# One ring of eight PSUM banks and new engine orders in the middle layers of a four-stage transformer kernel

## The chip, the cores and the metric

One core of a Trainium2 chip runs the whole program. The metric is the device time of one execution in microseconds, the median of several runs. A core has a matrix engine (TensorE, PE in the rows), VectorE (DVE), ScalarE (ACT), GpSimd (POOL) and SyncE (SP), which only issues transfers here. TensorE writes its products to PSUM, a memory of eight banks; VectorE and ScalarE read them there, and only then can a bank be written again.

## The reference

Two sequences of 2048 tokens of width 256 go through four blocks; everything is float32. The middle two blocks, which the change touches, are one function applied twice with other weights:

```python
def _layer(x, wqkv, qs, ksc, wo, lg, lb, w1, b1, w2, b2):
    h = shift_token(x)                      # right half of the features one token later
    q, k, v = jnp.split(h @ wqkv, 3, axis=-1)        # 8 heads of 64
    q = l2norm(q) * qs
    k = l2norm(k) * ksc
    q, k = rotary_xpos(q, k)
    o = local_attention(q, k, v)            # each 128-token window sees itself and the last one
    x = x + o @ wo
    h = layernorm(shift_token(x)) * lg + lb
    a, g = jnp.split(h @ w1 + b1, 2, axis=-1)        # 682 each
    return x + (a * gelu(g)) @ w2 + b2
```

Ahead of them stands an attention layer with 16 narrow heads and its own feed-forward, behind them a gated attention unit and a matmul with ternary weights.

## The kernel before

Each block is a phase of its own, with all engines joined at its end. The middle layers are the function `layer_b`, built once and run twice by a hardware loop. It walks over 16 tiles of 128 tokens (`t`), for both sequences (`b` is 0 or 1). To keep float32 accuracy TensorE forms most products as three: each operand is split in a high and a low part (`product3`, lines 113 to 115). The split of an operand that comes out of PSUM takes one operation on ScalarE (`_hi`) and one on VectorE (`_lo`), so nearly every matmul result is read by both.

The work of a tile is cut into stages, and every engine has its own list of them, `order[engine]`, with entries (stage, batch or part, shift). `in_turns` runs such a list once per turn i; an entry handles tile i + shift, and is left out where that tile doesn't exist. So a turn has work of up to six tiles in it, and the list is the order of the engine's instructions, fixed when the program is built. The stages on TensorE are: `turn_h` transposes the input; `project_k`, `project_q`, `project_v` are the three projections (6 matmuls of 512 columns each); `turn_qk` transposes k and q; `scores` and `scores2` form the scores of the first and the second four heads (64 rows are contracted, two matmuls side by side, 12 in all for each stage); `turn_p` and `turn_p2` transpose the probabilities; `values` multiplies them with v; `turn_o` and `out` bring the result through the output weights; `turn_f`, `up` 0 to 5 and `down` are the feed-forward. 33 entries and 344 matmuls stand in a full turn. Between them work, among others: on ScalarE the squares of q and k (L1242), the exponentials (L1273), the gelu of `up` (L1307) and the `_hi` parts; on VectorE `sums` (L1334), `spin` (the rotation, L1346 and L1348), the masked maxima of the scores (L1378), copies of the turned probabilities (L1399), `up` (L1449) and `mid` (L1458), the moments and the normalisation; on GpSimd the inverse norms by a power (L1195, L1209) and the sums and products on k and q (L1198 to L1206). SyncE issues the transfers to and from memory.

The exponential and the gelu need different function tables on ScalarE. Where one follows the other, the built program has an ACT_TABLE_LOAD.

The banks are given out by `Ring`. It numbers its uses in the order of TensorE's list, and use n lies in bank n modulo the ring's length. `wait_bank` makes TensorE wait until the use before in the same bank is drained; `written` and `read` count up the bank's two semaphores. Before the change there are two rings:

```python
main = Ring(sem, psum, f"{name}_main", range(0, 6), [(t, (job, b)) for stage, t, b in turns(order["pe"], NT) ...])
ffn = Ring(sem, psum, f"{name}_ffn", range(6, 8), [(t, (f_jobs[stage], b)) for stage, t, b in turns(order["pe"], NT) ...])
```

`main` holds the 36 uses of attention in a turn: h, k, q, v, kT, qT, four of scores (s), four of turned probabilities (p), two of values (o), oT and wo, each for both batches. `ffn` holds nine: f, w0 to w5 and y for both batches.

Of the kernel before, what the change touches and what calls it, by code (L numbers as in the profile page):

```python
# [906 lines left out]
def layer_b(nc, io, psum, sem, layer):  # L907
# [11 lines left out]
        "pe": [("scores", 0, -1), ("up", 0, -3), ("up", 1, -3), ("project_v", 1, -1), ("turn_h", 0, 0), ("turn_qk", 1, -1),
               ("out", 1, -2), ("scores2", 0, -1), ("down", 0, -4), ("down", 1, -4), ("scores", 1, -1), ("turn_p", 0, -1),  # L920
               ("up", 2, -3), ("scores2", 1, -1), ("turn_p2", 0, -1), ("project_k", 0, 0), ("values", 0, -1),
               ("turn_p", 1, -1), ("up", 3, -3), ("turn_h", 1, 0), ("project_q", 0, 0), ("up", 4, -3), ("turn_p2", 1, -1),
               ("project_k", 1, 0), ("turn_o", 0, -1), ("values", 1, -1), ("up", 5, -3), ("turn_qk", 0, 0),
               ("project_q", 1, 0), ("turn_f", 0, -2), ("project_v", 0, 0), ("out", 0, -1), ("turn_o", 1, -1)],
        "dve": [("up", 5, -4), ("turn_qk", 0, -1), ("turn_f", 0, -3), ("sums_q", 1, -1), ("spin_q", 1, -1), ("out", 0, -2),
               ("mid", 4, -4), ("turn_o", 1, -2), ("scores", 0, -1), ("mid", 5, -4), ("up", 0, -3), ("turn_h", 0, 0),
               ("up", 1, -3), ("turn_qk", 1, -1), ("out", 1, -2), ("scores2", 0, -1), ("down", 0, -4), ("scores", 1, -1),
               ("turn_p", 0, -1), ("scores2", 1, -1), ("down", 1, -4), ("mid", 0, -3), ("moments", 0, -2), ("sums_k", 0, 0),
               ("spin_k", 0, 0), ("up", 2, -3), ("values", 0, -1), ("turn_h", 1, 0), ("turn_p", 1, -1), ("sums_q", 0, 0),
               ("spin_q", 0, 0), ("mid", 1, -3), ("sums_k", 1, 0), ("up", 3, -3), ("spin_k", 1, 0), ("norm", 0, -2),  # L930
               ("mid", 2, -3), ("up", 4, -3), ("mid", 3, -3), ("turn_o", 0, -1), ("values", 1, -1)],
        "sp": [("out", 1, -2), ("scores2", 0, -1), ("residual", 1, -1), ("rope", 0, 0), ("load_r", 0, -3),
               ("residual", 0, -1), ("load_f", 0, -2), ("load_f", 1, -2), ("scores2", 1, -1), ("values", 1, -1),
               ("load_r", 1, -3), ("values", 0, -1), ("down", 0, -4), ("down", 1, -4), ("out", 0, -1)],
        "pool": [("moments", 0, -3), ("project_k", 0, -1), ("project_q", 0, -1), ("project_k", 1, -1), ("load_r", 0, -4),
                ("project_q", 1, -1), ("rope", 0, 0)],
    }
# [1511 lines left out]
```

How the kernel before makes its waits and increments, by code:

```python
    def wait_bank(self, eng, it, job):  # L63
        bank, use = self.place[job]
        eng.wait_ge(self.drained[bank], it * self.uses[bank] + use)
# [1 line left out]
    def wait_before(self, eng, it, job):  # L67
        bank = self.place[job][0]
        eng.wait_ge(self.drained[bank], it * self.uses[bank])
# [1 line left out]
    def wait_before_full(self, eng, it, job):  # L72
        bank = self.place[job][0]
        eng.wait_ge(self.full[bank], it * self.uses[bank])
# [1 line left out]
    def wait_full(self, eng, it, job):  # L77
        bank, use = self.place[job]
        eng.wait_ge(self.full[bank], it * self.uses[bank] + use + 1)
# [1 line left out]
    def wait_drained(self, eng, it, job):  # L81
        bank, use = self.place[job]
        eng.wait_ge(self.drained[bank], it * self.uses[bank] + use + 1)
# [18 lines left out]
    def link(self, ins):  # L102
        self.n += 1
        ins.then_inc(self.sem, 1)
        self.eng.wait_ge(self.sem, self.it * self.per_step + self.n)
# [42 lines left out]
    def wait_bank(self, eng, t, job):  # L148
        bank, use = self.place[t, job]
        if use > 0:
            eng.wait_ge(self.drained[bank], use)
# [1 line left out]
    def wait_full(self, eng, t, job):  # L153
        bank, use = self.place[t, job]
        eng.wait_ge(self.full[bank], use + 1)
# [1 line left out]
    def wait_drained(self, eng, t, job):  # L157
        bank, use = self.place[t, job]
        eng.wait_ge(self.drained[bank], use + 1)
# [24 lines left out]
    def link(self, ins):  # L184
        self.n += 1
        ins.then_inc(self.sem, 1)
        self.eng.wait_ge(self.sem, self.n)
# [555 lines left out]
        @block.tensor  # L743
        def _(pe):
            pe.wait_ge(consts_ready, n_consts + 1)
```

## Time and profile before

| | |
|---|---|
| median of 3 runs | 2870.94 us (2868.68 to 2872.28) |
| the profiled execution | 2867.2 us |
| its span, first to last instruction | 2865.4 us |
| granted clock of TensorE, mean | 0.954 of 2.4 GHz |
| busy: TensorE, VectorE, ScalarE, GpSimd | 2633.9, 2071.1, 1449.6, 1022.7 us |
| first layer | 0 to about 589 us |
| middle layers, weights and ramps included | about 589 to 1323 and 1323 to 2060 us |
| gated unit and ternary matmul | the rest |

Busy times of the engines overlap. A TensorE that counts as busy all the time can still lose time, since matmuls overlap in their pipeline: what it gets done shows in the distances between their starts, and the views below are read that way.

### The profile page before, as it was taken

To read this page: it belongs to the slowest core of one execution; us is meant where nothing else is said; L and a number is where in the kernel's file an instruction comes from. 1 tells how busy PE (TensorE), PEld (TensorE's weight loads), DVE (VectorE), ACT (ScalarE), POOL (GpSimd) and SP (SyncE) were. 2 spreads that over 40 slices of the span, in tenths; PEclk is the share of its full clock that TensorE was granted. 3 is DMA by queue.
4 is the path that set the end of the run, shared out by engine and by line. 5 is a ranking of instruction groups with operands and counts; after the bars stand their busy time and mean duration, and the time that the engine had idled before them with its cause. 6 is when DMAs were issued, how large, how long until landed. Compare 5 with 4: busy or idle time off the path is not lost. (4 is left out here: it accounts for less than half of the span.)

```text
span 2865.4 us, 57375 instructions
## 1 busy us (share of the span) xinstructions
PE 2633.9 (92%) x20450; PEld 2383.0 (83%) x20450; DVE 2071.1 (72%) x6161; ACT 1449.6 (51%) x3028; POOL 1022.7 (36%) x906
## 2 busy tenths in 40 slices
...
GB/s 71 32 33 41 33 33 33 33 99 89 64 87 79 77 78 79 84 79 90 75 79 87 66 90 78 76 80 73 108 129 98 23 30 30 71 128 30 30 30 23
DMA packets 223102, 189.55 MB, mean 66 GB/s; under 512 B 22357, under 2 KB 204505, under 8 KB 221913
## 3 DMA queue, kind: packets, MB, share of 16 engines
...
q8 instruction: 169, 2.77, 0.4%
...
## 5 line engine op out<-in xcount | busy, mean ns | idle before, releaser
L2147 ACT ACTIVATE c_sb_kern_hi<-c_sb_kern 128x512 fp32r<-128x512 f32 x128 | 80.9, 632 | 427.5 <-DVE c_sb_kern L2167 427.5
L2124 POOL TENSOR_TENSOR c_sb_kern_lo<-c_sb_kern,c_sb_kern_hi 128x512 fp32r<-128x512 f32 x128 | 166.8, 1304 | 313.4 <-ACT c_sb_kern_hi L2147 313.4
L2163 DVE SCALAR_TENSOR_TENSOR c_sb_kern<-psum,cu_bias 128x512 f32<-128x512 f32 x128 | 88.4, 690 | 245.8 <-PE psum L115 244.2
L1273 ACT ACTIVATE b_sb_probs<-b_sb_probs,b_sb_neg_top,b_sb_r_norm 128x256 f32<-128x256 f32 x512 | 262.3, 589 | 1.0 <-DVE b_sb_neg_top L1385 0.5
L1378 DVE CUSTOM_DVE_ANT_0 b_sb_probs<-psum,b_sb_mask 128x256 f32<-128x256 f32 x512 | 194.9, 417 | 65.0 <-PE psum L1520 64.0
L113 PE MATMUL psum<-b_sb_fT_lo,b_sb_w_hi 128*128 128x256 f32 x768 | 227.2, 296 | 4.1 <-DVE b_sb_fT_lo L1443 2.8
L115 PE MATMUL psum<-b_sb_fT_hi,b_sb_w_hi 128*128 128x256 f32 x768 | 216.5, 282 | 0.0
L114 PE MATMUL psum<-b_sb_fT_hi,b_sb_w_lo 128*128 128x256 f32 x768 | 215.8, 281 | 0.0
L113 PE MATMUL psum<-c_sb_kern_lo,cu_v_hi 128*128 128x512 f32 x512 | 206.9, 404 | 2.9 <-POOL c_sb_kern_lo L2124 2.9
L115 PE MATMUL psum<-c_sb_kern_hi,cu_v_hi 128*128 128x512 f32 x512 | 204.0, 398 | 0.0
L114 PE MATMUL psum<-c_sb_kern_hi,cu_v_lo 128*128 128x512 f32 x512 | 203.5, 398 | 0.0
L1565 PE MATMUL psum<-b_sb_v_now,b_sb_pT 128*128 128x65 f32 x1024 | 198.0, 275 | 0.0
L1564 PE MATMUL psum<-b_sb_v_prev,b_sb_pT 128*128 128x65 f32 x1024 | 194.5, 272 | 0.0
L1307 ACT ACTIVATE b_sb_gate<-psum,b_sb_b 128x256 f32<-128x256 f32 x192 | 91.0, 475 | 173.6 <-PE psum L115 162.2
L1206 POOL TENSOR_TENSOR b_sb_qk_cos<-b_sb_qk_cos,b_sb_qk_sin 128x512 f32<-128x512 f32 x64 | 82.2, 1284 | 250.2 <-DVEq L1350 250.2
L113 PE MATMUL psum<-b_sb_w_lo,b_sb_hT_hi 128*128 128x512 f32 x384 | 166.2, 433 | 4.5 <-DVE b_sb_hT_lo L1327 4.2
L1564 PEld LDWEIGHTS psum<-b_sb_v_prev,b_sb_pT 128*128 128x128 f32 x1024 | 157.7, 192 | 2.8
L507 ACT ACTIVATE a_probs<-a_probs,a_neg_top 128x128 f32<-128x128 f32 x512 | 155.1, 392 | 5.7 <-DVE a_neg_top L649 5.5
L1565 PEld LDWEIGHTS psum<-b_sb_v_now,b_sb_pT 128*128 128x128 f32 x1024 | 155.5, 192 | 0.0
L113 PEld LDWEIGHTS psum<-b_sb_fT_lo,b_sb_w_hi 128*128 128x128 f32 x768 | 144.7, 188 | 10.2 <-DVE b_sb_fT_lo L1443 3.3
L114 PE MATMUL psum<-b_sb_w_hi,b_sb_hT_lo 128*128 128x512 f32 x384 | 152.7, 398 | 0.0
L115 PE MATMUL psum<-b_sb_w_hi,b_sb_hT_hi 128*128 128x512 f32 x384 | 152.7, 398 | 0.0
...
## 6 DMA issues: line engine op xcount, KB each, us to landing
...
Y<-b_sb_y SPq DMA_DIRECT2D x128, 128.0 KB, 1.7
b_sb_h_in<-Y ACTq DMA_DIRECT2D x128, 64.0 KB, 1.9
...
b_sb_x_f<-Y SPq DMA_DIRECT2D x128, 64.0 KB, 2.1
...
```

The lines of the kernel that those rows point to most:

```text
L113: pe.matmul(out, w_hi, x_lo, start=first, stop=False)
L114: pe.matmul(out, w_lo, x_hi, start=False, stop=False)
L115: return pe.matmul(out, w_hi, x_hi, start=False, stop=last)
L507: ins = act.activation(probs[b][:, h, :], probs[b][:, h, :], ACT.Exp, bias=neg_top[b][:, h:h + 1], scale=float(A_HD) ** -0.5)
L1206: pool.tensor_tensor(q, q, qk_sin[b][:, 0, :, :], ALU.add).then_inc(qk_ready[b], 1)
L1273: ins = act.activation(probs[b][:, n, :], probs[b][:, n, :], ACT.Exp, bias=neg_top[b][:, n:n + 1], scale=r_norm[b][:, h:h + 1])
L1307: act.activation(gate[m % 2][:], ffn.out(t, ("w", m), 512)[:, 0:256], ACT.Gelu, bias=b1[:, 2 * m:2 * m + 1])\
L1378: ins = dve.tensor_tensor_reduce(out=probs[b][:, n, :], in0=main.out(t, (f"s{m}", b), 512)[:, j * 256:(j + 1) * 256], in1=mask[:, min(t, 1 ...
L1564: pe.matmul(out, pT[b][:, 2 * slot, :], v_prev[b][:, h, :], start=True, stop=False)
L1565: ins = pe.matmul(out, pT[b][:, 2 * slot + 1, :], v_now[b][:, h, :], start=False, stop=True)
L2124: pool.tensor_tensor(kern_lo[n][:], kern[n][:], kern_hi[n][:].bitcast(F32), ALU.subtract)\
L2163: sbanks.read(dve.scalar_tensor_tensor(out=kern[n][:], in0=sbanks.out((t, j), C_CHUNK), scalar=float(C_S) ** -0.5, in1=unit.bias[:, at:at ...
```

## The change

All of it lies in `layer_b`. The two rings become one of eight banks, numbered through all 45 uses of a turn in TensorE's order, and each call of `main` or `ffn` becomes one of `ring`. No stage is added, removed or changed, and no operation on data. The five lists of orders are other ones: the entries are the same, but their places and shifts differ. The core of the diff:

```diff
-               ("scores", 0, -2), ("mid", 0, -4), ("scores2", 0, -2), ("scores", 1, -2), ("mid", 1, -4), ("turn_p2", 0, -2),
+               ("mid", 5, -4), ("scores", 0, -1), ("up", 0, -3), ("up", 1, -3), ("scores2", 0, -1), ("mid", 0, -3),
...
-        "pe": [("scores", 0, -1), ("up", 0, -3), ("up", 1, -3), ("project_v", 1, -1), ("turn_h", 0, 0), ("turn_qk", 1, -1),
...
+        "pe": [("down", 1, -5), ("scores", 1, -2), ("scores2", 1, -2), ("turn_p", 0, -2), ("turn_p2", 0, -2),
...
-        f_jobs = {"turn_f": "f", "up": "w", "down": "y"}
-        main = Ring(sem, psum, f"{name}_main", range(0, 6), [(t, (job, b)) for stage, t, b in turns(order["pe"], NT)
-                                                             if stage in jobs for job in jobs[stage]])
-        ffn = Ring(sem, psum, f"{name}_ffn", range(6, 8), [(t, (f_jobs[stage], b)) for stage, t, b in turns(order["pe"], NT)
-                                                           if stage in f_jobs])
+        jobs.update(turn_f=["f"], up=["w"], down=["y"])
+        ring = Ring(sem, psum, f"{name}_ring", range(8), [(t, (job, b)) for stage, t, b in turns(order["pe"], NT)
+                                                          if stage in jobs for job in jobs[stage]])
```

The whole turn on TensorE now reads: `down` 1, `scores` 1, `scores2` 1, `turn_p` 0, `turn_p2` 0, `project_k` 0, `up` 2, `turn_p` 1, `project_q` 0, `up` 3, `values` 0, `turn_p2` 1, `project_k` 1, `values` 1, `turn_o` 0, `project_q` 1, `project_v` 0, `up` 4, `turn_o` 1, `turn_qk` 0, `project_v` 1, `turn_h` 0, `up` 5, `turn_f`, `turn_h` 1, `out` 1, `scores` 0, `turn_qk` 1, `scores2` 0, `out` 0, `up` 0, `up` 1, `down` 0.

TensorE, at the scores of batch 1, in a full turn (numbers behind names are the batch). Before, they stand between `down` of batch 1 and the turned probabilities of batch 0, and `up` 2 follows:

```order
L115 MATMUL psum<-b1_sb_w2_hi,b1_sb_mid_hi 128x256
L1520 MATMUL psum<-b1_sb_kT_lo1,b1_sb_qT_hi1 128x256 x2
L1520 MATMUL psum<-b1_sb_kT_hi1,b1_sb_qT_lo1 128x256 x2
L1520 MATMUL psum<-b1_sb_kT_hi1,b1_sb_qT_hi1 128x256 x2
L1520 MATMUL psum<-b1_sb_kT_lo1,b1_sb_qT_hi1 128x256 x2
L1520 MATMUL psum<-b1_sb_kT_hi1,b1_sb_qT_lo1 128x256 x2
L1520 MATMUL psum<-b1_sb_kT_hi1,b1_sb_qT_hi1 128x256 x2
L1541 MATMUL psum<-b1_sb_ident,b1_sb_probs0 128x128 x8
L113 MATMUL psum<-b1_sb_fT_lo,b1_sb_w1_hi 128x256
L114 MATMUL psum<-b1_sb_fT_hi,b1_sb_w1_lo 128x256
L115 MATMUL psum<-b1_sb_fT_hi,b1_sb_w1_hi 128x256
```

After, the rows begin inside the first of two scores stages of batch 1 and end with the projection of k:

```order
L1519 MATMUL psum<-b1_sb_kT_hi1,b1_sb_qT_lo1 128x256 x2
L1519 MATMUL psum<-b1_sb_kT_hi1,b1_sb_qT_hi1 128x256 x2
L1519 MATMUL psum<-b1_sb_kT_lo1,b1_sb_qT_hi1 128x256 x2
L1519 MATMUL psum<-b1_sb_kT_hi1,b1_sb_qT_lo1 128x256 x2
L1519 MATMUL psum<-b1_sb_kT_hi1,b1_sb_qT_hi1 128x256 x2
L1519 MATMUL psum<-b1_sb_kT_lo1,b1_sb_qT_hi1 128x256 x2
L1519 MATMUL psum<-b1_sb_kT_hi1,b1_sb_qT_lo1 128x256 x2
L1519 MATMUL psum<-b1_sb_kT_hi1,b1_sb_qT_hi1 128x256 x2
L1540 MATMUL psum<-b1_sb_ident,b1_sb_probs0 128x128 x16
L113 MATMUL psum<-b1_sb_w_lo,b1_sb_hT_hi0 128x512
```

The second four heads' scores moved up to the first four's, and both halves of batch 0's probabilities are turned behind them.

ScalarE, from the exponentials of batch 0 on. Before:

```order
L1273 ACT_TABLE_LOAD
L1273 ACTIVATE b_sb_probs<-b_sb_probs,b_sb_neg_top,b_sb_r_norm 128x256 x4
L1314 ACTIVATE b_sb_mid_hi<-b_sb_mid 128x256
L1273 ACTIVATE b_sb_probs<-b_sb_probs,b_sb_neg_top,b_sb_r_norm 128x256 x8
L1314 ACTIVATE b_sb_mid_hi<-b_sb_mid 128x256
L1287 ACTIVATE b_sb_pT<-psum 128x512 x2
L1242 ACTIVATE b_sb_qk_sin<-psum 128x512
L1273 ACTIVATE b_sb_probs<-b_sb_probs,b_sb_neg_top,b_sb_r_norm 128x256 x4
L1307 ACT_TABLE_LOAD
L1307 ACTIVATE b_sb_gate<-psum,b_sb_b 128x256
L1235 ACTIVATE b_sb_hT_hi<-psum 128x256
```

After:

```order
L1272 ACT_TABLE_LOAD
L1272 ACTIVATE b_sb_probs<-b_sb_probs,b_sb_neg_top,b_sb_r_norm 128x256 x4
L1306 ACT_TABLE_LOAD
L1306 ACTIVATE b_sb_gate<-psum,b_sb_b 128x256 x2
L1272 ACT_TABLE_LOAD
L1272 ACTIVATE b_sb_probs<-b_sb_probs,b_sb_neg_top,b_sb_r_norm 128x256 x4
L1313 ACTIVATE b_sb_mid_hi<-b_sb_mid 128x256
L1272 ACTIVATE b_sb_probs<-b_sb_probs,b_sb_neg_top,b_sb_r_norm 128x256 x8
L1241 ACTIVATE b_sb_qk_sin<-psum 128x512
L1313 ACTIVATE b_sb_mid_hi<-b_sb_mid 128x256
L1286 ACTIVATE b_sb_pT<-psum 128x512 x2
```

The first two gelus of `up` moved between the two halves of batch 0's exponentials, with a table load on either side.

VectorE, around the sums and the spin of batch 0's k (`squares0`, `qk_cos0`). Before:

```order
L1458 TENSOR_TENSOR b1_sb_mid_lo<-b1_sb_mid0,b1_sb_mid_hi 128x256
L1427 BN_STATS b1_sb_stats<-b1_sb_x_f 128x6 x2
L1430 BN_AGGR b1_sb_mv<-b1_sb_stats 128x2 x2
L1432 TENSOR_SCALAR b1_sb_var<-b1_sb_mv 128x2
L1334 TENSOR_REDUCE b1_sb_squares0<-b1_sb_qk_sin0 128x8
L1335 TENSOR_SCALAR b1_sb_squares0<-b1_sb_squares0 128x8
L1346 TENSOR_TENSOR b1_sb_qk_sin0<-psum,b1_sb_rope 128x8x32 x2
L1348 TENSOR_TENSOR b1_sb_qk_cos0<-psum,b1_sb_rope 128x512
L1449 SCALAR_TENSOR_TENSOR b1_sb_mid0<-psum,b1_sb_b1,b1_sb_gate0 128x256
```

After:

```order
L1333 TENSOR_REDUCE b1_sb_squares0<-b1_sb_qk_sin0 128x8
L1334 TENSOR_SCALAR b1_sb_squares0<-b1_sb_squares0 128x8
L1345 TENSOR_TENSOR b1_sb_qk_sin0<-psum,b1_sb_rope 128x8x32 x2
L1347 TENSOR_TENSOR b1_sb_qk_cos0<-psum,b1_sb_rope 128x512
L1457 TENSOR_TENSOR b1_sb_mid_lo<-b1_sb_mid0,b1_sb_mid_hi 128x256
L1426 BN_STATS b1_sb_stats<-b1_sb_x_f 128x6 x2
L1429 BN_AGGR b1_sb_mv<-b1_sb_stats 128x2 x2
L1431 TENSOR_SCALAR b1_sb_var<-b1_sb_mv 128x2
L1448 SCALAR_TENSOR_TENSOR b1_sb_mid0<-psum,b1_sb_b1,b1_sb_gate0 128x256
```

The low part of `mid` and the moments moved from ahead of the sums to behind the spin, ahead of `up` 2.

## Rows read from the trace of the kernel before

**Rows 1.** Busy time by stretches: stretch, length, busy us (instructions) of each engine, clock, DMA.
```profile
612.00:700.00 88.00, 73.83 (x538) 63.55 (x539) 67.01 (x206) 43.56 (x82) 48.98 (x42) 0.92 0.21 65
700.00:1250.00 550.00, 549.26 (x4449) 512.30 (x4447) 467.31 (x1350) 331.43 (x640) 221.82 (x169) 1.00 0.25 78
1250.00:1323.00 73.00, 61.56 (x522) 59.37 (x520) 39.08 (x110) 29.37 (x62) 5.37 (x5) 0.97 0.21 65
```

**Rows 2.** Waits of TensorE, 700 to 1250 us: total, times, longest.
```profile
PE psum L1541 <- ACT b_sb_probs L1273: 0.7, 2, 0.4
```

**Rows 3.** Timeline of TensorE: start, us, line, operation, shapes, count.
```profile
904.26 0.38 PE L1520 MATMUL psum<-b_sb_kT_lo,b_sb_qT_hi 64*128 64x256 f32 x2
...
911.90 0.28 PE L115 MATMUL psum<-b_sb_wo_hi,b_sb_oT_hi 128*128 128x256 f32 x1
912.11 0.39 PE L1520 MATMUL psum<-b_sb_kT_lo,b_sb_qT_hi 64*128 64x256 f32 x2
912.33 0.28 PE L1520 MATMUL psum<-b_sb_kT_hi,b_sb_qT_lo 64*128 64x256 f32 x2
...
912.81 0.28 PE L1520 MATMUL psum<-b_sb_kT_hi,b_sb_qT_hi 64*128 64x256 f32 x2
913.02 0.39 PE L113 MATMUL psum<-b_sb_w_lo,b_sb_mid_hi 128*128 128x256 f32 x1
913.24 0.28 PE L114 MATMUL psum<-b_sb_w_hi,b_sb_mid_lo 128*128 128x256 f32 x1
...
924.08 0.33 PE L1564 MATMUL psum<-b_sb_v_prev,b_sb_pT 128*128 128x65 f32 x2
...
927.60 1.04 PE L1541 MATMUL psum<-b_sb_ident,b_sb_probs 128*128 128x128 f32 x8
```

**Rows 4.** The same view, one turn later.
```profile
946.71 0.39 PE L1520 MATMUL psum<-b_sb_kT_lo,b_sb_qT_hi 64*128 64x256 f32 x2
```

**Rows 5.** The same view, in the ramp of the first middle layer.
```profile
670.93 0.28 PE L1520 MATMUL psum<-b_sb_kT_hi,b_sb_qT_hi 64*128 64x256 f32 x2
671.05 0.29 PE L1520 MATMUL psum<-b_sb_kT_lo,b_sb_qT_hi 64*128 64x256 f32 x2
671.18 0.28 PE L1520 MATMUL psum<-b_sb_kT_hi,b_sb_qT_lo 64*128 64x256 f32 x2
```

**Rows 6.** Groups of VectorE, 750 to 1200 us: busy, mean ns, idle before.
```profile
L1378 DVE CUSTOM_DVE_ANT_0 b_sb_probs<-psum,b_sb_mask 128x256 f32<-128x256 f32 x166 | 63.1, 417 | 24.6 <-PE psum L1520 24.3
L1458 DVE TENSOR_TENSOR b_sb_mid_lo<-b_sb_mid,b_sb_mid_hi 128x256 fp32r<-128x256 f32 x64 | 46.2, 722 | 4.3 <-DVE b_sb_mid L1449 2.7
L1346 DVE TENSOR_TENSOR b_sb_qk_sin<-psum,b_sb_rope 128x256 f32<-128x256 f32 x86 | 32.2, 416 | 2.6 <-DVE b_sb_mid L1449 2.6
L1449 DVE SCALAR_TENSOR_TENSOR b_sb_mid<-psum,b_sb_b,b_sb_gate 128x256 f32<-128x256 f32 x64 | 30.7, 480 | 13.4 <-ACT b_sb_gate L1307 12.7
L1348 DVE TENSOR_TENSOR b_sb_qk_cos<-psum,b_sb_rope 128x512 f32<-128x512 f32 x43 | 29.2, 679 | 0.0
L1334 DVE TENSOR_REDUCE b_sb_squares<-b_sb_qk_sin 128x8 f32<-128x512 f32 x43 | 29.2, 678 | 0.4
L1399 DVE COPY b_sb_pT<-psum 128x512 f32<-128x512 f32 x44 | 28.2, 681 | 0.0
```

**Rows 7.** Timelines of VectorE and GpSimd (POOL).
```profile
918.61 0.42 DVE L1378 CUSTOM_DVE_ANT_0 b_sb_probs<-psum,b_sb_mask 128x256 f32<-128x256 f32 x1 [2.38 <-PE psum L1520]
...
934.69 1.28 POOL L1206 TENSOR_TENSOR b_sb_qk_cos<-b_sb_qk_cos,b_sb_qk_sin 128x512 f32<-128x512 f32 x1 [4.10 <-DVEq L1350]
...
934.70 1.55 DVE L1458 TENSOR_TENSOR b_sb_mid_lo<-b_sb_mid,b_sb_mid_hi 128x256 fp32r<-128x256 f32 x1
```

**Rows 8.** Timeline of ScalarE, a table switch and what follows.
```profile
911.96 1.28 ACT L1273 ACT_TABLE_LOAD   x1
913.25 2.08 ACT L1273 ACTIVATE b_sb_probs<-b_sb_probs,b_sb_neg_top,b_sb_r_norm 128x256 f32<-128x256 f32 x4
...
926.91 1.28 ACT L1307 ACT_TABLE_LOAD   x1
```

More of the change, by code:

```diff
@@ L919, in layer_b @@
-        "pe": [("scores", 0, -1), ("up", 0, -3), ("up", 1, -3), ("project_v", 1, -1), ("turn_h", 0, 0), ("turn_qk", 1, -1),
[L920 to L936, printed above, removed]
+        "act": [("turn_p2", 0, -2), ("up", 2, -4), ("load", 0, 0), ("load", 1, 0), ("project_q", 0, -1), ("up", 3, -4),
+               ("turn_p2", 1, -2), ("project_k", 1, -1), ("turn_o", 0, -2), ("project_q", 1, -1), ("project_v", 0, -1),
+               ("turn_o", 1, -2), ("mid", 2, -4), ("turn_qk", 0, -1), ("up", 4, -4), ("turn_h", 0, 0), ("project_v", 1, -1),
+               ("mid", 3, -4), ("turn_h", 1, 0), ("turn_f", 0, -3), ("up", 5, -4), ("mid", 4, -4), ("turn_qk", 1, -1),
+               ("mid", 5, -4), ("scores", 0, -1), ("up", 0, -3), ("up", 1, -3), ("scores2", 0, -1), ("mid", 0, -3),
+               ("scores", 1, -1), ("scores2", 1, -1), ("project_k", 0, 0), ("mid", 1, -3)],
@@ new lines, in layer_b @@
+        "pe": [("down", 1, -5), ("scores", 1, -2), ("scores2", 1, -2), ("turn_p", 0, -2), ("turn_p2", 0, -2),
+               ("project_k", 0, -1), ("up", 2, -4), ("turn_p", 1, -2), ("project_q", 0, -1), ("up", 3, -4),
+               ("values", 0, -2), ("turn_p2", 1, -2), ("project_k", 1, -1), ("values", 1, -2), ("turn_o", 0, -2),
+               ("project_q", 1, -1), ("project_v", 0, -1), ("up", 4, -4), ("turn_o", 1, -2), ("turn_qk", 0, -1),
+               ("project_v", 1, -1), ("turn_h", 0, 0), ("up", 5, -4), ("turn_f", 0, -3), ("turn_h", 1, 0), ("out", 1, -2),
+               ("scores", 0, -1), ("turn_qk", 1, -1), ("scores2", 0, -1), ("out", 0, -2), ("up", 0, -3), ("up", 1, -3),
+               ("down", 0, -4)],
```

221 lines of the change are left out of this document (114 added, 107 removed).

## Prediction

> **What bounds the kernel now.** I read the busy time by stretches first. The middle layers run twice, at about 612 to 1323 and 1346 to 2050 us. Between the ends of the first one TensorE is busy 549.3 of 550 us at a granted clock of 1.00, the full 2.4 GHz, while VectorE works 467 and ScalarE 331 [rows 1]. The waits of that stretch hold one entry for TensorE, 0.7 us in all [rows 2]. So nothing but TensorE sets the pace there. The same group of matmuls, scores of batch 0, begins at 904.26 and at 946.71 [rows 3, 4]: a turn, one step of 128 tokens of both batches, takes 42.45 us, and 16 of them 679 us. A change of the banks cannot win back waits that are not there. What can be won in a full turn is the time that TensorE loses between its own groups; what can be won elsewhere lies at the two ends of a layer, where TensorE is idle 88 - 73.8 = 14.2 us (part of it before the first load has landed) and 73 - 61.6 = 11.4 us [rows 1].
>
> **Where TensorE loses time between groups.** The scores contract over 64 rows, all else over 128. Inside a run of 256-column matmuls the starts are 0.12 apart. From the last `out` matmul at 911.90 to the first scores pair at 912.11 it is 0.21, and from that to the second pair at 912.33 it is 0.22; leaving, 912.81 to 913.02 is 0.21 and the next step, to 913.24, 0.22 [rows 3]. So entering costs 0.09 + 0.10 and leaving 0.09 + 0.10: 0.19 each way. In the ramp of the layer two scores groups do stand next to each other: 670.93, 671.05, 671.18 are 0.12 and 0.13 apart [rows 5], so joined groups pay nothing at the seam. The Trainium skill ("TensorEngine Tiling (Array Packing)", Tiling Modes, Key Properties) says that changing the tiling mode, not just the tile, drains TensorE; these rows agree in kind and give the size.
>
> **Part one, the order on TensorE.** Before, the four scores groups of a turn stand alone: four entries, four exits. After, scores and scores2 of batch 1 follow each other between `down` and the turning of the probabilities: three entries and three exits. The lost pair is one entry from and one exit to full-row matmuls, 0.19 + 0.19 = 0.38 us in a turn. The matmuls themselves are the same 344 in a turn; the other seams change place and I cost them at 0, plus or minus 0.05. 32 turns by 0.38 = 12.2 us less. All of it lies on the path, since TensorE is the path.
>
> **Part two, the ring.** Now use n waits until use n-8 is drained, whatever it is, where projections and attention had six and the feed-forward two. With 45 uses a turn this is no new work, but it ties the chains of the feed-forward to the attention. I walked one turn by the new order with TensorE never waiting, time 0 at the start of `down` of batch 1, with group lengths from TensorE's timeline (values 924.08 to 927.60 = 3.52, a scores group 912.11 to 913.02 = 0.91 [rows 3], the others likewise). VectorE, one engine in order, gets the scores of batch 1 at 3.3. Two sets of four (0.42 each [rows 6], with the small ones about 1.8 a set) bring it to 6.9, the two copies for batch 0 (0.61 apart, 0.68 long [rows 6]) to 8.1. The copies of batch 1 wait for TensorE's turning, written at 9.2, and end at 10.4. Sums of squares (0.68 and a short one) to 11.2; spin, twice 0.42 and 0.68 and its signal, to 12.8; `mid` 0 to 14.2 (below); moments, about 1.1, to 15.3; `up` 2, 0.48, to 15.8 [rows 6]. The bank of w2 is the one that p3 of batch 1 takes eight uses later, and TensorE wants that at 16.1: a margin of 0.3 us, the smallest in the turn. Next are h of batch 1 after w4 (about 31.0 against 30.3: 0.7), scores of batch 0 after kT and qT (32.7 against 31.8: 0.9), and some of 1 to 2 us. So I take no wait: 0. The other end is all of these late by the one thing that I can size badly, below.
>
> **VectorE's room.** In the old turn it waits 2.38 us at 918.61 for the scores [rows 7] and some 1.1 us elsewhere; in the new one a turn is 0.38 shorter and its work the same, so about 3 us stay. One cost moves: at 934.70 a `mid` subtraction takes 1.55 us where the undisturbed ones take 0.42, because a GpSimd addition began at 934.69 and lasted 1.28 [rows 7]; the mean over the stretch is 0.72 [rows 6]. The new order puts `mid` 0 behind spin_k of batch 0, exactly the place where spin lets the GpSimd addition start, and I have counted 1.1 us for it in the 15.8. The wide normalisation keeps its place behind a spin.
>
> **Part three, ScalarE.** The new order puts `up` 0 and 1 between the exponentials of batch 0's two halves: four table switches in a turn in place of two, at 1.28 us [rows 8]: +2.6 us a turn. ScalarE is busy 331 of 550 us [rows 1], 25.6 in a turn; 28.2 of 42 is still no bound. What hangs on it: the exponentials of scores2 of batch 0, done by 2.4 in my walk and wanted by TensorE at 5.2; and `up` 2, which ScalarE has ready at about 11.8, while VectorE comes to it at 15.3. Both are covered, with 2.8 and 3.5 us; beyond that each us late is a us per turn. In the trace the exponential starts 1.29 after its load began, at once [rows 8]. The Trainium skill ("ScalarE: Activation LUTs", What ACT_TABLE_LOAD costs) adds a drain of about 1380 ns to each switch and tells to do all of one set before the next; by it the extra would be 5.3 us a turn and the cover of 2.8 would be nearly gone, so it speaks against this change. The sum goes by the rows, where the drain isn't seen.
>
> **The ends of a layer.** The first turn of the new order turns both h before the first projection, so the projection of k of batch 1 doesn't wait for VectorE; but the chain through spin, GpSimd and the k and q turning is as long as before. From walking it I take 1 us less a layer, between 4 less and 3 more, of the 25.6 idle [rows 1]. The last turns hold the same `turn_f` to `up` seam as before: 0.
>
> **SyncE and GpSimd.** Their orders change, but each transfer in my walk lands well ahead (k and v are moved about 20, wanted at 27): 0. Outside the middle layers nothing moves.
>
> **The sum.** The profiled execution took 2867.2 us (span 2865.4), 3.7 under the median of 2870.9 of three runs. 2867.2 - 12.2 - 2 by 1 = 2853.0; against the median, 2856.7, or 0.5% less.
>
> **Rivals.**
> - *A bank comes late in every turn (slower).* w2's drain passes 16.1. The cause would be a second block of VectorE by a GpSimd addition in the chain from 3.3 to 15.8, at 1.1 us (1.55 - 0.42 [rows 7]). As VectorE waits for TensorE again at the next `down`, the wait recurs in all turns. One block more: 1.1 - 0.3 = 0.8 us a turn, less the 0.38: +0.42 by 32 = +13 us, less the 2 at the ends: 2882 us; it decides from a chain 0.7 us longer than mine. For it: margins of 0.3 and 0.7 are thin and eight banks now tie everything. Against: the GpSimd additions fall behind the spins only, and between 9.2 and 10.4 VectorE waited anyway. The same price, at 2.8 us, would hold for ScalarE's late exponentials.
> - *Small waits eat the gain (same).* The chain is late by 0.5 us: 0.2 us a turn is lost, 6 us back: 2863, or with 0.4, 2869.
> - *The seam isn't saved.* The 0.12 of the joined pair is seen in one ramp turn of each layer; where the second group has to wait for a bank just drained the seam stays at 0.2. Then only half or none of 12.2 comes: 2863 to 2869.
> - *The ends give more.* If the two feed-forward banks held the ramp up, up to 5 us a layer go: 2847.
>
> **How the numbers follow.** Forecast 0.62 (2850 to 2862). Small waits or a seam not saved 0.20, of which half falls within 0.2% (5.7 us, about what a measurement can tell here from no change) of 2870.9. The ends give more 0.07. A bank late in every turn 0.11. Faster by more than that: 0.62 + 0.10 + 0.07 = 0.79; same 0.10; slower 0.11. The range goes from the ends giving more, 2846, to small waits eating all, 2869.
>
> **What the profile after would show.** Right: full turns 42.0 to 42.1 apart at clock 1.00; no wait of TensorE between them; in the scores of batch 1 starts 0.12 apart through all twelve pairs; 60 more ACT_TABLE_LOADs, about 77 us more of ScalarE, waited for by nobody. Wrong: a repeated TensorE wait for `b_sb_mid` L1448 at the turning of the probabilities (a bank), or for `b_sb_probs` (exponentials late), once a turn; or seams of 0.2 inside the joined pair.

## The result

| | before | after |
|---|---|---|
| median | 2874.36 us (2868.68 to 2877.38, 8 runs) | 2862.84 us (2858.58 to 2865.82, 8 runs) |
| profiled execution | 2867.2 us | 2859.99 us |
| its span | 2865.4 us | 2858.2 us |

The ratio of after to before is 0.996, with a 95% interval of 0.9949 to 0.9971: the changed kernel is faster by 0.4%, some 11.5 us. The forecast was 14 us less, 2857, in a range of 2846 to 2869.

The busy times in the middle of the first layer, the same view as [rows 1] (stretch, length, busy us of each engine, granted clock, DMA):

```profile
700.00:1250.00 550.00, 548.93 (x4495) 515.51 (x4493) 458.82 (x1372) 359.93 (x668) 210.80 (x168) 1.00 0.25 78
```

TensorE is the bound as before, 548.9 of 550 us at full clock. But in the same 550 us it now has 4495 matmuls in place of 4449: 1% more of its work. Its waits, 720 to 1250 us (total, times, longest):

```profile
PE psum L1480 <- DVE b_sb_mid L1448: 0.2, 1, 0.2
```

One wait in twelve turns. The joined scores of batch 1 in TensorE's timeline (start, us, line, operation, shapes, count), with the first matmul of the same group one turn later:

```profile
918.41 0.28 PE L115 MATMUL psum<-b_sb_w_hi,b_sb_mid_hi 128*128 128x256 f32 x1
918.62 0.39 PE L1519 MATMUL psum<-b_sb_kT_lo,b_sb_qT_hi 64*128 64x256 f32 x2
918.84 0.28 PE L1519 MATMUL psum<-b_sb_kT_hi,b_sb_qT_lo 64*128 64x256 f32 x2
...
919.20 0.28 PE L1519 MATMUL psum<-b_sb_kT_hi,b_sb_qT_lo 64*128 64x256 f32 x2
919.32 0.28 PE L1519 MATMUL psum<-b_sb_kT_hi,b_sb_qT_hi 64*128 64x256 f32 x2
...
920.04 0.28 PE L1519 MATMUL psum<-b_sb_kT_hi,b_sb_qT_hi 64*128 64x256 f32 x2
920.25 1.97 PE L1540 MATMUL psum<-b_sb_ident,b_sb_probs 128*128 128x128 f32 x16
...
960.67 0.39 PE L1519 MATMUL psum<-b_sb_kT_lo,b_sb_qT_hi 64*128 64x256 f32 x2
```

The entry is there (0.21, 0.22) and the exit (0.21), and in between all steps are 0.12: the second group, which begins at 919.32, pays neither. The turn is 960.67 - 918.62 = 42.05 us, against 42.45 [rows 3, 4]; over seven turns of each the difference is 0.407.

The length of a layer is read from the start of its first matmul to that of its last. After:

```profile
621.29 0.45 PE L1480 MATMUL psum<-b_sb_ident,b_sb_h_in 128*128 128x128 f32 x1 [8.46 <-DMA b_sb_h_in<-Y]
...
1310.43 0.28 PE L115 MATMUL psum<-b_sb_w_hi,b_sb_mid_hi 128*128 128x256 f32 x1
...
1351.07 0.45 PE L1480 MATMUL psum<-b_sb_ident,b_sb_h_in 128*128 128x128 f32 x1 [8.61 <-DMA b_sb_h_in<-Y]
...
2039.21 0.28 PE L115 MATMUL psum<-b_sb_w_hi,b_sb_mid_hi 128*128 128x256 f32 x1
```

Before, the same four:

```profile
619.66 0.66 PE L1481 MATMUL psum<-b_sb_ident,b_sb_h_in 128*128 128x128 f32 x2 [8.58 <-DMA b_sb_h_in<-Y]
...
1313.82 0.28 PE L115 MATMUL psum<-b_sb_w_hi,b_sb_mid_hi 128*128 128x256 f32 x1
...
1352.33 0.45 PE L1481 MATMUL psum<-b_sb_ident,b_sb_h_in 128*128 128x128 f32 x1 [8.55 <-DMA b_sb_h_in<-Y]
...
2046.42 0.28 PE L115 MATMUL psum<-b_sb_w_hi,b_sb_mid_hi 128*128 128x256 f32 x1
```

The first layer went from 694.16 to 689.14 us (-5.0), the second from 694.09 to 688.14 (-6.0), -11.0 together, close to the 11.5 between the medians. 16 turns by 0.407 would be -6.5 in each, so the ends gave back 1.5 and 0.5. The stretch between the layers, in which the weights are loaded, was 38.5 us before and 40.6 after, and the first layer began 1.6 us later. In the traces of the other kernels, whatever their orders, the stretch took 39.0 to 41.1 us and the first layer began at 617.2 to 624.0, so I take both for the spread of single executions. They are why the profiled execution came out only 7.2 us shorter (11.0 - 2.1 - 1.6).

### The profile page after: what moved, and what is told of

It is laid out like the page before. It is cut to its first block and busy times, and to the rows that moved or that the text cites. A ratio compares the mean times of both kernels' runs of the same rounds, so it can differ in the third digit from the quotient of the medians.

```text
span 2858.2 us, 57407 instructions
## 1 busy us (share of the span) xinstructions
PE 2624.7 (92%) x20450; PEld 2385.3 (83%) x20450; DVE 2046.6 (72%) x6161; ACT 1501.8 (53%) x3080; POOL 1000.6 (35%) x906
## 5 line engine op out<-in xcount | busy, mean ns | idle before, releaser
L1194 POOL TENSOR_TENSOR b_sb_r_norm<-b_sb_squares,b_sb_power 128x8 f32<-128x8 f32 x64 | 105.0, 1641 | 643.8 <-DVE b_sb_squares L1334 643.8
L113 PE MATMUL psum<-b_sb_fT_lo,b_sb_w_hi 128*128 128x256 f32 x768 | 218.9, 285 | 2.9 <-DVE b_sb_fT_lo L1442 2.9
L114 PEld LDWEIGHTS psum<-b_sb_fT_hi,b_sb_w_lo 128*128 128x128 f32 x768 | 144.6, 188 | 3.5
```

Source lines behind the costliest of these rows:

```text
L113: pe.matmul(out, w_hi, x_lo, start=first, stop=False)
L114: pe.matmul(out, w_lo, x_hi, start=False, stop=False)
L1194: pool.tensor_tensor(r, s, p, ALU.pow).then_inc(r_ready[1][b], 1)
```

## The experiments

Two questions: is the one saved seam the whole gain, and what do the ring and the other orders do? The theory is that the seam is all of it and the ring gives nothing of itself; the rival, that the shared banks take waits away.

**x1_split: the changed kernel without the joined pair.**

```diff
-        "pe": [("down", 1, -5), ("scores", 1, -2), ("scores2", 1, -2), ("turn_p", 0, -2), ("turn_p2", 0, -2),
+        "pe": [("down", 1, -5), ("scores", 1, -2), ("turn_p", 0, -2), ("scores2", 1, -2), ("turn_p2", 0, -2),
```

> The changed kernel with one thing undone: on TensorE scores2 of batch 1 goes back behind the turning of the first half of batch 0's probabilities, so the two scores groups stand apart again. Ring of eight and all other orders stay. Theory (the seam is the whole gain): one entry and one exit come back, 0.38 us a turn, a full turn 42.43 in place of 42.05, 32 turns: +12.2 us, so about 2862.8 + 12.2 = 2875, level with the kernel before. Rival (the gain came from the ring and the new orders taking waits away elsewhere): a turn stays near 42.05 and the time near 2863.

Measured 2872.79 us; ratio to before 1.000 (0.9991 to 1.001). TensorE's timeline, the first group of the pair in two turns:

```profile
878.45 0.39 PE L1519 MATMUL psum<-b_sb_kT_lo,b_sb_qT_hi 64*128 64x256 f32 x2
...
920.85 0.39 PE L1519 MATMUL psum<-b_sb_kT_lo,b_sb_qT_hi 64*128 64x256 f32 x2
```

A turn takes 42.40 us, 0.35 more than after, and all of the gain is gone. This is also the price of everything else in the change, the ring, the two more table loads of ScalarE and the five new lists: 42.40 against 42.45, nothing that the times can tell. Its layers took 694.67 and 694.05 us, those of the kernel before 694.16 and 694.09.

**x2_join_only: the kernel before with the joined pair.**

```diff
-               ("out", 1, -2), ("scores2", 0, -1), ("down", 0, -4), ("down", 1, -4), ("scores", 1, -1), ("turn_p", 0, -1),
-               ("up", 2, -3), ("scores2", 1, -1), ("turn_p2", 0, -1), ("project_k", 0, 0), ("values", 0, -1),
+               ("out", 1, -2), ("scores2", 0, -1), ("down", 0, -4), ("down", 1, -4), ("scores", 1, -1), ("scores2", 1, -1),
+               ("turn_p", 0, -1), ("up", 2, -3), ("turn_p2", 0, -1), ("project_k", 0, 0), ("values", 0, -1),
```

> The kernel before with one thing done: on TensorE scores2 of batch 1 is moved up behind scores of batch 1. Two rings of six and two and all the other lists as before. Theory (seam): the turn falls from 42.45 to 42.07, 32 turns: -12.2 us, so 2874.4 - 12.2 = 2862, as good as the changed kernel without any ring of eight. VectorE waits for the turned probabilities of batch 0 up to 0.9 us longer, inside the 2.4 us that it waits there anyway. Rival (the joined groups need the new ring or the new VectorE order, else a bank comes late): the gain is eaten, 2868 to 2880, and a repeated TensorE wait shows at the turned probabilities.

Measured 2875.26 us; ratio 1.001 (1.0001 to 1.0019). The theory alone is wrong here: the seam inside the pair is saved, but the full turns vary from 42.35 to 42.83 and average 42.50. TensorE's timeline shows what eats it, at the projection of k of batch 0, in two turns:

```profile
971.81 0.47 PE L113 MATMUL psum<-b_sb_w_lo,b_sb_hT_hi 128*128 128x512 f32 x1 [0.47 <-ACT b_sb_pT L1287]
...
1014.33 0.47 PE L113 MATMUL psum<-b_sb_w_lo,b_sb_hT_hi 128*128 128x512 f32 x1 [0.16 <-DVE b_sb_top L1378]
```

and VectorE's timeline why: the maxima of the second pair (L1378), which drain s2's bank, come behind the two copies.

```profile
969.70 1.28 DVE L1399 COPY b_sb_pT<-psum 128x512 f32<-128x512 f32 x2
...
971.24 0.42 DVE L1378 CUSTOM_DVE_ANT_0 b_sb_probs<-psum,b_sb_mask 128x256 f32<-128x256 f32 x1
```

In a ring of six, k of batch 0 takes the bank of s2 of batch 1, drained at 971.24 + 0.42 = 971.66; k starts at 971.81. (The first of the two waits is put down to ScalarE; the second names the maxima.) The turns in which the profile shows no wait lose by it too: at 928.97 this projection starts 0.26 us after the start of the last turned probability, where in the kernel before it is 0.03. That is too small to show as idle, since one matmul's time overlaps the next.

**x2b_join_dve: the same, with VectorE's scores2 of batch 1 ahead of the copies.**

```diff
-               ("turn_p", 0, -1), ("scores2", 1, -1), ("down", 1, -4), ("mid", 0, -3), ("moments", 0, -2), ("sums_k", 0, 0),
+               ("scores2", 1, -1), ("turn_p", 0, -1), ("down", 1, -4), ("mid", 0, -3), ("moments", 0, -2), ("sums_k", 0, 0),
```

> The kernel before with two things done: scores2 of batch 1 behind scores of batch 1 on TensorE (as in the run x2_join_only), and the same on VectorE, ahead of the copies of the turned probabilities. Still two rings of six and two. Theory (x2_join_only lost its 0.38 us because s2 of batch 1, whose bank k of batch 0 takes six uses later, was drained behind the copies): the bank comes 1.4 us earlier, the wait at the projection of k goes, a full turn is 42.07, 32 turns: -12 us against before, about 2860. Rival (six banks can't carry the joined pair): the wait stays or moves to the values, the turn stays 42.4 to 42.5 and the time at 2871 to 2875.

Measured 2879.55 us; ratio 1.0029 (1.0019 to 1.0039): slower than before. The wait at the projection is gone, as the theory had it, and the quietest turns are 42.14, 0.31 under the kernel before, where 42.07 was expected. But the copies are now later than `values` wants them (a TensorE wait of 0.3 us for `b_sb_pT` L1399 in the trace), so the turns reach 42.7, and the ramp and the last turns lose more than the full ones gain: turns 1 and 2 (a layer's first is turn 0) take 31.1 and 31.4 us in place of 30.2 and 30.2, turn 16 takes 35.1 and 38.4 in place of 34.1. So the small edit isn't the change. The saved seam needs the engines' orders around it; whether some other order on two rings would carry it is not tested.

**x3_ring8_old: the one ring of eight with the old orders** (against the kernel before, the lists of uses cut).

```diff
-        main = Ring(sem, psum, f"{name}_main", range(0, 6), [...])
-        ffn = Ring(sem, psum, f"{name}_ffn", range(6, 8), [...])
+        ring = Ring(sem, psum, f"{name}_ring", range(8), [...])
```

> The one ring of eight with the five old lists of orders. From the times of the kernel before, each use's start against the drain of the use eight places earlier: four places a turn would be late, p2 of batch 0 behind y of batch 1 by 2.3 us, o0 of batch 1 behind w3 by 1.8, p0 of batch 1 behind w2 by 1.7, kT of batch 0 behind w4 by 1.1. Theory (the ring gives nothing by itself and needs other orders): TensorE waits at these places, 2.3 us a turn if one wait shifts the others away and 4 if half of them remain: +75 to +130 us, about 2950 to 3000. Rival (the ring alone is harmless or helps): within 5 us of the kernel before.

Measured 3116.37 us; ratio 1.0853 (1.0836 to 1.087). Slower than the forecast of at most 3000 by 116 us. TensorE's waits over some eleven turns, 720 to 1250 us:

```profile
PE psum L1539 <- DVE b_sb_y L1463: 24.1, 10, 2.4
PE psum L1562 <- DVE b_sb_mid L1447: 19.6, 11, 1.8
PE psum L1539 <- DVE b_sb_mid L1447: 16.7, 10, 1.7
```

Three of the four late places are there with the sizes read from the margins of before (2.4, 1.8, 1.7 against 2.3, 1.8, 1.7), and none covers another: 5.9 us a turn. The fourth, at kT, doesn't show. Between the starts of the matmuls the three places cost 6.2 us a turn (why that is more than the waits shown is told in the last section). The rest is the clock: by stretches, the granted clock (third column from the end) falls behind the third wait to its lower level of 1.2 GHz, for 6.8 us in all:

```profile
870.00:880.00 10.00, 8.22 (x60) 7.44 (x59) 7.71 (x15) 4.72 (x10) 4.26 (x3) 1.00 0.05 13
880.00:885.00 5.00, 5.00 (x28) 5.00 (x28) 4.50 (x11) 0.00 (x0) 3.04 (x3) 0.56 0.02 5
885.00:890.00 5.00, 5.00 (x28) 4.64 (x28) 1.94 (x4) 2.12 (x5) 1.29 (x1) 0.76 0.53 187
```

The full turns take about 50.3, 52.0 or 54.8 us, and in the clock's records of these turns it stands at 1.2 GHz for 3.4 us behind the second wait, for 6.8 behind the third, and in the longest for 13.7 in three pieces. 42.45 + 6.2 is 48.7; the 1.6, 3.3 and 6.1 us above it go with the lower clock.

**x4_rings62_new: the new orders on the two old rings** (the swap, against the changed kernel's list for VectorE).

```diff
-               ("down", 0, -4), ("up", 0, -3), ("up", 1, -3), ("down", 1, -4), ("scores", 1, -1), ("scores2", 1, -1),
+               ("up", 0, -3), ("up", 1, -3), ("down", 0, -4), ("down", 1, -4), ("scores", 1, -1), ("scores2", 1, -1),
```

> The new lists of orders on the two old rings, with one swap on VectorE without which two banks can't carry them: up 0 and up 1 go ahead of down of batch 0, since y of batch 0 now waits for the bank of w0. Theory (the new orders need the shared banks): y of batch 0 begins when VectorE has used w0, at about 915.75 in place of 914.26 of the changed kernel's turn, 1.5 us late each turn; k of batch 0 waits for s2 of batch 1 some 0.4 more. Turn 43.6 to 44.0, +50 to +60 us against the changed kernel, 2910 to 2925. Rival (the ring is not needed): the turn stays at 42.05 and the time at 2863.

Measured 2925.0 us; ratio 1.0179 (1.0162 to 1.0196). TensorE's waits:

```profile
PE psum L113 <- DVE b_sb_mid L1450: 14.7, 12, 1.3
PE psum L113 <- DVE b_sb_top L1379: 2.7, 12, 0.2
PE psum L1521 <- DVE b_sb_y L1423: 2.1, 12, 0.2
```

Once a turn each: y of batch 0 for w0's bank (14.7 / 12 = 1.2 us, where 1.5 was forecast), k for s2's, and s3 for wo's, which was not foreseen. The turn is 44.17, a little over the 43.6 to 44.0 expected, and the time is at the upper edge of its range. These orders cost 1.8% on two rings, and by x3_ring8_old the ring costs 8.5% with the old orders. Together they come to zero, and leave room for the joined pair.

**z1_vector_1us: how much room is there for a late bank?** The changed kernel with work added on VectorE:

```diff
                 dve.wait_ge(mid_hi_ready, t * B_FC + m + 1)
+                for k in range(3 if m == 0 else 0):
+                    dve.tensor_reduce(scratch[k][:], mid[m % 2][:], AX.X, ALU.add)
```

> The changed kernel with three sums of a 128x256 tile added on VectorE ahead of the subtraction of mid 0 (their results go nowhere), some 0.35 us each, 1.05 in all: the one block more of the prediction's slower rival. By the prediction's walk the bank of w2 had 0.3 us to spare: 0.75 us a turn, +24 us, 2887. By the drains seen in the trace after, w2's bank has 1.5 us to spare and the smallest margins are h of batch 1 after w4 with 0.8, and kT, qT for the scores of batch 0 with 1.0: 0.3 us a turn, +9 us, about 2872, with the wait at the turning of h. If VectorE's room takes it up before: 2863.

Measured 2875.5 us; ratio to before 1.0009 (0.9996 to 1.0022), by the ratios some 14 us more than after. TensorE's timeline at the turning of h of batch 1, after first and then this run, and the run's waits:

```profile
946.93 0.60 PE L1590 MATMUL psum<-b_sb_ident,b_sb_xn 128*128 128x128 f32 x4
947.36 0.38 PE L1480 MATMUL psum<-b_sb_ident,b_sb_h_in 128*128 128x128 f32 x2
...
947.80 0.60 PE L1593 MATMUL psum<-b_sb_ident,b_sb_xn 128*128 128x128 f32 x4
948.56 0.41 PE L1483 MATMUL psum<-b_sb_ident,b_sb_h_in 128*128 128x128 f32 x2 [0.16 <-DVE b_sb_mid L1449]
```

```profile
PE psum L1483 <- DVE b_sb_mid L1449: 2.0, 12, 0.2
```

The wait comes where the drains of the trace had it, at h after w4, in each turn, and not at w2's bank. The turns are 42.49 us. The wait itself shows 0.16 and the turn grew by 0.44: 0.33 at this place (0.76 from start to start in place of 0.43) and the rest at the turning of the probabilities.

The edit did somewhat more than 1.05 us at first. The three sums took 0.99, and behind them the subtraction of `mid` 0 started while GpSimd's addition ran and in most turns took 0.91 us in place of 0.43, so VectorE came 1.4 us later to `up` 2, which drains w2's bank; from `mid` 1 on it was 1.0 behind. That w2's bank still came in time says that its margin was at least 1.4.

**z2_two_loads: what is left of ScalarE's cover?** The changed kernel with one more switch there and back:

```diff
             def up(t, m):
+                if m == 1:
+                    act.activation(scratch[:], ident[:, 0:1], ACT.Exp)
```

> The changed kernel with an exponential of one column added on ScalarE between up 0 and up 1, which brings two more table loads, 2.56 us and some 0.2 each for the small ones, to where the change had put two: it asks how much of the cover is left, and whether a switch costs more than its load. In the trace after, the exponentials of scores2 of batch 0 end 2.2 us before TensorE turns them. Theory (a switch costs its 1.28 us alone): 2.8 - 2.2 = 0.6 us a turn, and up 1 comes about as late for VectorE: +20 us, 2883. Rival (by the Trainium skill, ScalarE: Activation LUTs, a drain of about 1380 ns goes with each switch): 2 x 1.38 more, 3.4 us a turn, +108 us, 2971.

Measured 2882.47 us; ratio 1.0034 (1.0023 to 1.0045). ScalarE's timeline:

```profile
966.06 1.28 ACT L1306 ACT_TABLE_LOAD   x1
967.35 0.20 ACT L1306 ACTIVATE b_sb_scratch<-b_sb_ident 128x1 f32<-128x1 f32 x1
967.56 1.28 ACT L1309 ACT_TABLE_LOAD   x1
968.86 0.47 ACT L1309 ACTIVATE b_sb_gate<-psum,b_sb_b 128x256 f32<-128x256 f32 x1
969.35 1.28 ACT L1273 ACT_TABLE_LOAD   x1
```

Each load takes 1.28 us, what follows starts within 0.02, and each load starts within 0.02 of the end before it. The drain that the Trainium skill ("ScalarE: Activation LUTs", What ACT_TABLE_LOAD costs) puts beside each switch isn't in this trace, and the time is nowhere near the 2971 that it would have given. The turn is 42.40, TensorE waits 0.2 us a turn for the exponentials (L1273) and each full turn is 0.35 longer: of the 2.8 us added ScalarE's cover took some 2.4. Turn 4 of the layers, the last before the full ones, grew by 5.2 and 4.1 us: TensorE waits 3.5 us there in place of 0.6, and behind that wait the granted clock stood at 1.2 GHz for 6.8 and 3.4 us.

**r1_ramp, y2_join_both, y4_mixed, y5_mixed_ramp: the ends, and more of the same.**

r1_ramp moves one entry on VectorE, in the first turn of a layer:

```diff
+            steps.remove(("turn_qk", 0, 0))
+            steps.insert(steps.index(("sums_q", 0, 1)), ("turn_qk", 0, 0))
```

> The changed kernel with one thing moved in the first turn of a layer: on VectorE the low parts of kT and qT of batch 0 of the first tile come ahead of the sums and spin of q of batch 1. It takes away the longest wait in the ramp: TensorE stood 2.8 us, from 636.1 to 638.9, ahead of the first scores. Theory A (that wait is what the ends lost): the first scores come at about 636.8, 2.1 us less a layer, 4 us in all, 2859 in place of 2863. Theory B (the ramp is set by GpSimd's chain of k and q of batch 1, whose last sum ends at 640.7 whatever VectorE does): the wait moves to the turning of k and q of batch 1, the first scores of batch 1 stay within 0.4 us of 22.0 us after the layer's first matmul, and the whole gives 0 to 1 us.

Measured 2864.34 us; ratio 0.9968 (0.9958 to 0.9979): no gain on the changed kernel. TensorE's longest wait in the ramp, first of after in the view of its waits from 620 to 650 us, then of r1_ramp in the timeline:

```profile
PE psum L1519 <- DVE b_sb_qT_lo L1369: 2.5, 1, 2.5
```

```profile
638.71 0.39 PE L1524 MATMUL psum<-b_sb_kT_lo,b_sb_qT_hi 64*128 64x256 f32 x2 [3.32 <-DVE b_sb_qk_cos L1347]
```

The operands are there earlier: counted from the layer's first matmul, the low part of qT ends at 14.8 us in place of 17.5. Yet the scores start at 17.9 in place of 17.6. Neither theory had this: the releaser is now the last product of spin (L1347). The scores' second bank is, eight uses back, that of q of batch 1, which spin drains. So VectorE has to do both, the low part of qT and the spin of q of batch 1, before the first scores can start, and which comes first changes nothing. Theory B was right in that the first scores of batch 1 stayed in their place, at 22.1 and 22.0, without any gain.

y2_join_both joins the other two scores groups as well:

```diff
-               ("scores", 0, -1), ("turn_qk", 1, -1), ("scores2", 0, -1), ("out", 0, -2), ("up", 0, -3), ("up", 1, -3),
+               ("scores", 0, -1), ("scores2", 0, -1), ("turn_qk", 1, -1), ("out", 0, -2), ("up", 0, -3), ("up", 1, -3),
```

> The changed kernel with the other pair of scores joined as well: scores2 of batch 0 directly behind scores of batch 0 on TensorE, the turning of k and q of batch 1 behind both, the same on VectorE, and on ScalarE that turning behind mid 5; up 5 ahead of turn_f on ScalarE and VectorE, since s3 of batch 0 now takes the bank of w5, which was drained at 949.77 where TensorE would want it at 949.95. Theory (each joined pair is worth an entry and an exit): turn 42.05 - 0.38 = 41.67, 32 turns: -12.2 us, about 2851. Rival (the margins are used up, a bank or the exponentials come late): a repeated wait of TensorE of 0.3 us or more a turn, 2858 or more.

Measured 2866.09 us; ratio 0.9977 (0.9968 to 0.9986). The full turns did fall to 41.66 us with no new wait, -0.39 as expected. But the ramp and the end gave it back: turn 1 took 21.6 us in place of 19.7, turn 2 31.7 to 32.7 in place of 30.1 to 30.4, turn 18 17.7 in place of 15.5. In the ramp, TensorE's waits of 636 to 706 us:

```profile
PE psum L1519 <- DVE b_sb_qT_lo L1369: 6.9, 3, 2.5
```

Three in place of one, in turns that are half empty. Of the 2.3 us that turn 18 lost 0.8 is a wait; for the rest the clock's records show 1.2 GHz for 3.4 us in it, in both layers. y4_mixed therefore uses these lists in turns 3 to 16 alone:

```diff
+            for stage, b, shift in (full if 3 <= i <= 16 else order)[key]:
```

> The lists of the run y2_join_both (both pairs of scores joined) in the turns 3 to 16 of a layer, and those of the changed kernel in the turns before and behind. In y2_join_both a full turn took 41.66 in place of 42.05, but turns 1 and 2 lost 1.9 and 1.5 to 2.2 and turn 18 lost 2.3, which took all of it back. Expected if these losses come from the order of the turns that show them: turn 3 -1.0, turn 4 -0.4, twelve turns by -0.39 = -4.7, a layer -6.1 and both -12 us: a ratio to the kernel before of 0.992, about 2850. Rival (the change of lists between turns costs a wait of its own, or the bank numbers shift into late ones): half of it or less, 2857 or more.

Measured 2849.35 us (2841.3 to 2856.29, 6 runs); ratio 0.9918 (0.99 to 0.9935), as expected, and below the interval of the changed kernel. So the losses did come from the lists of the end turns. TensorE's timeline, the scores of batch 0 with no seam at 942.99 to 943.11, and the scores of batch 1 in two turns, 41.66 apart:

```profile
911.83 0.39 PE L1541 MATMUL psum<-b_sb_kT_lo,b_sb_qT_hi 64*128 64x256 f32 x2
...
942.99 0.28 PE L1541 MATMUL psum<-b_sb_kT_hi,b_sb_qT_hi 64*128 64x256 f32 x2
943.11 0.28 PE L1541 MATMUL psum<-b_sb_kT_lo,b_sb_qT_hi 64*128 64x256 f32 x2
...
953.49 0.39 PE L1541 MATMUL psum<-b_sb_kT_lo,b_sb_qT_hi 64*128 64x256 f32 x2
```

Its layers took 683.3 and 683.7 us. y5_mixed_ramp adds the edit of r1_ramp to it.

> y4_mixed and r1_ramp together. Expected is the sum of the two: by theory B of r1_ramp 0 to 1 us under y4_mixed, about 2850; by theory A 4 us under it, 2846.

Measured 2853.26 us; ratio 0.9931 (0.9918 to 0.9944). The intervals of y4_mixed and y5_mixed_ramp overlap: the ramp edit adds nothing that can be told, as in r1_ramp.

## Why the prediction was right, and where it wasn't

**The seam, -12.2 us: right.** 0.38 was forecast from four distances in one timeline; x1_split prices it at 0.35 and y2_join_both prices a second one at 0.39. The turn fell by 0.41, and the 0.05 that x1_split leaves may be the other seams, which the prediction had at 0 plus or minus 0.05. The rule cited beside it (the Trainium skill, "TensorEngine Tiling (Array Packing)", Key Properties) names the drain; the runs give its size, and that it is paid again for each group.

**The ring, 0: right in sum, wrong in one margin.** The smallest margin was to be w2's bank with 0.3 us. With VectorE 1.4 us later there (z1_vector_1us) that bank still was in time, and h after w4, forecast with 0.7, was the late one. The step that failed is the 1.1 us block by GpSimd, "counted in the 15.8": it hardly ever comes. VectorE's and GpSimd's timelines after, in an ordinary turn, and in the one turn with a wait:

```profile
929.02 0.42 DVE L1457 TENSOR_TENSOR b_sb_mid_lo<-b_sb_mid,b_sb_mid_hi 128x256 fp32r<-128x256 f32 x1
...
927.76 1.64 POOL L1194 TENSOR_TENSOR b_sb_r_norm<-b_sb_squares,b_sb_power 128x8 f32<-128x8 f32 x1 [22.78 <-DVE b_sb_squares L1334]
929.36 1.27 POOL L1197 TENSOR_TENSOR b_sb_qk_cos<-b_sb_qk_cos,b_sb_qk_sin 128x512 f32<-128x512 f32 x1
...
1097.55 1.54 DVE L1457 TENSOR_TENSOR b_sb_mid_lo<-b_sb_mid,b_sb_mid_hi 128x256 fp32r<-128x256 f32 x1 [0.50 <-DVE b_sb_qk_cos L1347]
...
1097.55 1.27 POOL L1197 TENSOR_TENSOR b_sb_qk_cos<-b_sb_qk_cos,b_sb_qk_sin 128x512 f32<-128x512 f32 x1
```

I let GpSimd's addition start when spin ends (928.9). It starts at 929.36, since the power ahead of it in GpSimd's queue takes 1.64 us from 927.76, and `mid` 0 has begun 0.34 before. In the other turn, number 13 of both layers, `mid` 0 began 0.5 us after the spin in place of 0.15 and met the addition: 1.54 us, VectorE over 1 us behind, and the wait below. Of the 32 of `mid` 0 only these two met it. What held them up is open. Before it stood a transfer issue of ScalarE that took 1.90 us at 1093.74 where its neighbours take 0.33 to 0.46, but the one thing that this subtraction takes from ScalarE, the high part (L1313), ends at 1093.79, as far into the turn as in the one before. Turn 13 is as much longer in x1_split, y2_join_both and y4_mixed. The mean of all six `mid` subtractions fell from 722 [rows 6] to 498 ns over the same window: before, `mid` 1 took 1.55 us and `mid` 4 1.12 in nearly every turn, now they take 0.82 and 0.42. The new order takes VectorE away from GpSimd's additions, where the prediction had its work the same.

```profile
1093.38 0.41 ACT L1313 ACTIVATE b_sb_mid_hi<-b_sb_mid 128x256 fp32r<-128x256 f32 x1
...
1093.74 1.90 ACTq L1228 DMA_DIRECT2D b_sb_h_in<-Y  x1
...
1115.95 0.41 PE L1480 MATMUL psum<-b_sb_ident,b_sb_h_in 128*128 128x128 f32 x2 [0.16 <-DVE b_sb_mid L1448]
```

So the slower rival was sized too high: about one block more costs 0.44 us a turn and not 0.8, some 14 us back and level with the kernel before, not 2882. Its mechanism, a late bank by VectorE's chain with the wait in each turn, was as described; its place was not, h after w4 and not w2.

**VectorE's room, about 3 us: right.** Its largest wait of 720 to 1250 us:

```profile
DVE b_sb_y L1464 <- PE psum L115: 30.8, 24, 2.1
```

That is 2.4 us a turn at `down`; with the turned probabilities (11.4) it is 3.4, and with the scores (7.2) 3.9.

**ScalarE, 0: right.** 28.5 us more in 550 (359.9 against 331.4) and nobody waits. Over the whole program it has 52 more instructions, all of them table loads, and is busy 52.2 us longer, where 60 loads and 77 us were forecast. For its cover 2.8 us were forecast and z2_two_loads measures some 2.4.

**The ends, -1 us a layer: wrong in sign.** They cost 1.5 and 0.5, or 1.1 and 0.1 without the wait of turn 13. The step that failed is that turning both h early makes the ramp shorter. It did let the projection of k of batch 1 start earlier, 6.5 us after the layer's first matmul in place of 8.1. But the first scores came at 17.6 and 17.1 us in the two layers in place of 15.4: TensorE waits 2.5 us for the low part of qT, which VectorE makes behind the sums and the spin of q of batch 1. By the first scores of batch 1 (22.0 and 21.4, before 21.6) nothing was gained.

The walk also kept the clock at full speed. In the first layer after, some 20 us in, it stood at 1.2 GHz for 6.9 us. This is the granted clock (third column from the end) at the scores of batch 1:

```profile
643.00:648.00 5.00, 5.00 (x41) 4.62 (x40) 4.57 (x27) 4.99 (x10) 0.00 (x0) 0.59 0.17 54
```

In the second layer it was 1.00 there, and from these scores to the turned probabilities it took 1.2 us less, of which it then lost 0.9 waiting. What is left of that, 0.3, and 0.5 of later loads in the first turn are most of the 1.0 between the two layers. The clock's records show such a fall beginning 17 to 23 us into the layer in 12 of the 16 layers of the eight kernels here that run the new orders on one ring, and in neither layer of the kernel before.

**The sum.** -13 from 32 turns and +2 outside of them (0.9 of it the wait of turn 13 in both layers) make -11. The forecast of -14 had 0.8 too little in the turns and 4 too much in the rest, so its two errors partly cancel. The time alone would not have told the forecast from the rival of small waits, whose 2863 is the median measured; the turn of 42.05 with one wait in twelve does.
